# Layer-norm chunks prepared three ahead, a weight array padded to 128 rows, and the constants loaded in three parts, in a four-layer spectral kernel

## The chip, the cores and the metric

The kernel runs on one core of one Trainium2 chip, in fp32. The metric is the device time of one execution in microseconds (us), as the median of several runs. The engines are named as in the profile: PE (TensorE; PEld is its weight load), DVE (VectorE), ACT (ScalarE), POOL (GpSimd), SP (SyncE; its queue SPq issues the DMAs).

## The reference

`x` has the shape (2, 64, 64, 384). Four layers follow one another. Each takes a real 2-D FFT over the two image axes, multiplies blocks of 48 channels (8 blocks) by complex 48x48 weights twice, with an activation between, shrinks small values or not, transforms back and adds its input:

```
xf = rfft2(x)                                  # per layer
h  = act(clinear(xf, w1) + b1)                 # 8 blocks of 48 channels
y  = softshrink(clinear(h, w2) + b2)           # layers 0, 2, 3
x  = irfft2(y) + x
```

Layer 1 differs: its input is layer-normalised over the channels first, its activation is gelu, nothing is shrunk, the sum is `irfft2 + normalised x + x`, and a token MLP (384 to 1536 to 384, with a second layer norm) follows it.

## The kernel before, in words

All transforms are matmuls with constant matrices. The work unit is a **block** g of 48 channels: 8 for each layer, 32 in all. Two blocks form a **unit** of 96 channels (16 units), which is what one load of x, one store and one load of spectral weights bring. A layer-1 block is worked in 8 **steps** t, a block of the other layers in 9. A block's forward row transform f1 runs in 6 **chunks** of 8 channels, one block ahead of the rest.

PE's program is written out by hand. Step t of block g holds, in this order: m1 of step t-1 (first spectral matmul, L433), f6 (last inverse transform, L481) of an older block, f2 (forward column transform, L419) of step t, one chunk of f1 (L403) of block g+1 in the steps `f1_at` (0, 1, 3, 4, 6, 7 in layer 1), one chunk of f5 (L466) of block g-1 in the steps `f5_at` (1 to 6), and m2 of step t-1 (L449). DVE's program in a step is: the residual add of f6 (L764), the copy of m2's result to `u` (L744; L739 and L741 in the other layers), and in layer 1 `centre`.

`centre(n)` makes the normalised chunk n from x: it subtracts the mean (L796) and multiplies by the reciprocal deviation (L798), and writes slot n % 6 of the ring `xn`. Chunks 0 to 5 are made by ACT beforehand. When PE works f1 of chunk n0, DVE makes chunk n0+1 in that step, behind the `u` copy. It first waits until POOL is done with the slot: `keep(n-6)` waits for f1 of chunk n-6, multiplies the chunk by the gain (L965), adds it to x (L967) and signals `sum_ready`. Where a unit's x is needed for the first time, `centre` waits for its load too.

In layers 0, 2 and 3 POOL copies x into the ring instead (`turn`, L957), six chunks ahead of f1. POOL also prepares a unit's spectral weights (`weights`, L932 to L943, six instructions into `w0` or `w1`), in its own program order between chunks, after a wait for the load into `wstage`. That load (L275) brings the array `spectral`, which has 113 rows, to 113 partitions; the matmuls use up to 113 rows.

SP issues all DMAs from one queue, in program order. At the start: the first 128 columns of the constants (f1's matrix), the first 48 channels of unit 0 in two DMAs (`x_first`), the remaining constants, the weights of units 0 and 1, the other 48 channels of unit 0 in two DMAs, x of units 1 and 2, layer-norm rows and columns, parts of the MLP's first weights. POOL needs the other 48 channels of unit 0 for block 1, whose chunk 0 PE works in step 0 of block 0. Later, SP stores a finished unit, waits for the store, loads x three units on into the buffer, and then issues the weights load of the next unit.

Of the kernel before, what the change touches and what calls it, by code (L numbers as in the profile page):

```python
# [10 lines left out]
P = 128  # L11
BATCH, SIDE, CHANNELS = 2, 64, 384
BLOCKS, BLOCK = 8, 48
# [18 lines left out]
CHUNKS = BLOCK // CHAN  # L32
# [3 lines left out]
PART_ROWS = SIDE // PARTS  # L36
COLS = 8
RING = CHUNKS
STATS = PAIRS + 1

(C_D1, C_ID, C_D2, C_D2A, C_D2B, C_D5, C_D5H, C_D6) = [P * n for n in range(8)]
C_SIGN = 8 * P
C_COLS = C_SIGN + 5
ROWS = ONE_ROW + 1
MIX = SIDE + BLOCK
SECOND, BIAS = ROWS, ROWS + PAIR
W_COLS = BIAS + 1
# [39 lines left out]
def groups_before(g):  # L87

    return sum(LAYER[n // BLOCKS].n for n in range(g))
# [42 lines left out]
def build(nc, x, consts, spectral, lncols, ln1, cols, w1, w2, b2, out):  # L132
    with ExitStack() as ctx:
# [6 lines left out]
        def sem(name):  # L140
            return ctx.enter_context(nc.semaphore(name))
# [6 lines left out]
        const = sb("const", [P, C_COLS])  # L148
# [15 lines left out]
        with ExitStack() as scope:  # L164
# [15 lines left out]
            wstage = sb("wstage", [P, 2, 2, W_COLS])  # L180
# [30 lines left out]
        LAST_BANKS = (F5_BANK, M1_BANK)  # L211
        TURN_BANKS, MM1_BANKS, MM2_BANKS = (6, 7), (4, 5), (0, 1, 2, 3)

        s_first, s_const, s_wts = sem("s_first"), sem("s_const"), sem("s_wts")
        x_loaded = [sem(f"x_loaded{n}") for n in range(3)]
        stored = [sem(f"stored{n}") for n in range(3)]
        x_first = sem("x_first")
# [51 lines left out]
        def _(sp):  # L269

            def load_weights(unit):
                layer, i = unit // PAIRS, unit % PAIRS
                if unit >= 2:
                    sp.wait_ge(w_ready, W_STEPS * (unit - 1))
                sp.dma_start(wstage[0:ROWS, unit % 2, :, :],  # L275
                             spectral[layer].rearrange("(g k) p n -> p g k n", k=2)[:, i]
                             ).then_inc(w_loaded[unit % 2], 16)

# [5 lines left out]
            def load_unit(unit):  # L284
                for part in range(PARTS):
                    for b in range(BATCH):
                        load_rows(unit, b, part)
# [69 lines left out]
                    sp.wait_ge(m_stored[r], 16 * TILES // 2)  # L357
                load_rows(2 * PAIRS, 1, PARTS - 1)

            sp.dma_start(const[:, 0:C_ID], consts[:, 0:C_ID]).then_inc(s_first, 16)  # L360
            for n in range(2):
                sp.dma_start(xs[0][n * SIDE:(n + 1) * SIDE, :, 0:BLOCK], image(x, n, 0, SIDE, 0)[:, :, 0:BLOCK]
                             ).then_inc(x_first, 16)
            sp.dma_start(const[:, C_ID:], consts[:, C_ID:]).then_inc(s_const, 16)
            load_weights(0)
            load_weights(1)
            for n in range(2):
                sp.dma_start(xs[0][n * SIDE:(n + 1) * SIDE, :, BLOCK:PAIR], image(x, n, 0, SIDE, 0)[:, :, BLOCK:PAIR]
                             ).then_inc(x_loaded[0], 16 * PARTS)
            load_unit(1)  # L370
            load_unit(2)
            sp.dma_start(lnrow[:, :, :], ln1.rearrange("a c -> (a c)").partition_broadcast(P)
                         .rearrange("p (a c) -> p a c", a=2)).then_inc(s_wts, 16)
# [13 lines left out]
        def _(pe):  # L387
# [19 lines left out]
            def f2(g, t):  # L407

                L = layer_of(g)
                if t == 0:  # L410
                    pe.wait_ge(z_ready, CHUNKS * (g + 1))
                    if g == 0:
                        pe.wait_ge(s_const, 16)
                        pe.wait_ge(gap_clear, 1)
                start, size = L.groups[t]
                for n in range(size):
                    slot, col = L.column(start + n)
                    for a in range(2):
                        mm = pe.matmul(ps[a * SIDE:a * SIDE + BLOCK, F2_BANK, n * L.kh:(n + 1) * L.kh],  # L419
                                       z[:, g % 2, slot, :], basis(col + a * SIDE, L.kh), start=True, stop=True)  # L420
                mm.then_inc(f2_done, 1)
# [32 lines left out]
            def f5(g, k, bank=F5_BANK, reuse=1):  # L454

                L = layer_of(g)
                n = CHUNKS * g + k
                if k == 0:
                    pe.wait_ge(u_ready, groups_before(g + 1))
                    if L.norm and g % BLOCKS < 2:  # L460
                        pe.wait_ge(u_clear, 2)
                if n >= reuse:
                    pe.wait_ge(v_ready, n + 1 - reuse)
                for c in range(CHAN):
                    for a in range(2):
                        mm = pe.matmul(ps[a * SIDE:(a + 1) * SIDE, bank, c * SIDE:(c + 1) * SIDE],  # L466
                                       u[0:2 * L.kh, g % 2, k * CHAN + c, BATCH * a:BATCH * a + SPAN],
                                       const[0:2 * L.kh, (C_D5 if L.full else C_D5H) + a * SIDE:][:, 0:SIDE],
                                       start=True, stop=True)
                mm.then_inc(f5_done, 1)  # L470
# [256 lines left out]
        def _(dve):  # L727
# [82 lines left out]
            def spectral(first, last):  # L810
                norm = LAYER[first // BLOCKS].norm
                if norm:
                    centre(CHUNKS)
                for g in range(first, last):
                    L = layer_of(g)
                    for t in range(L.n):
                        done, k = rows_at(g, t)
                        if done >= first and k is not None:
                            f6(done, k)
                        if t:  # L820
                            m2(g, t - 1)
                        elif g > first:
                            m2(g - 1, layer_of(g - 1).n - 1)
                        if norm and t in L.f1_at:
                            n = CHUNKS * (g + 1 - first) + L.f1_at.index(t) + 1
                            if n < CHUNKS * (last - first):
                                centre(n)
                        if norm and 0 <= L.n * (g - last + 2) + t - 4 < HC:
                            split_first(L.n * (g - last + 2) + t - 4)
                g = last - 1  # L830
                for k in range(1, 4):
                    f6(g - 1, k)
                m2(g, layer_of(g).n - 1)
                for k in range(4, ROWCHUNKS):
                    f6(g - 1, k)
                for k in range(ROWCHUNKS):
                    f6(g, k)
# [78 lines left out]
        def _(pool):  # L916
# [79 lines left out]
            def spectral(first, last):  # L996
                for g in range(first, last):
                    for k in range(CHUNKS):
                        if layer_of(g).norm:
                            keep(CHUNKS * (g - first) + k)  # L1000
                        else:
                            turn(g, k)
                        if k == 2 and g % 2 and g > first + 1 and g + 1 < 4 * BLOCKS:
                            weights((g + 1) // 2)
                    if g == 0:
                        pool.wait_ge(s_const, 16)
                        weights(0)
                        weights(1)

            spectral(*SEGMENTS[0])  # L1010
# [15 lines left out]
def host_constants():  # L1026

    import numpy as np
    n, f = np.arange(SIDE), 2 * np.pi / SIDE
    half = np.arange(HALF)  # L1030

    col = np.stack([np.cos(f * np.outer(n, half)), -np.sin(f * np.outer(n, half))], 1)
    col[:, 1, 0] = (-1.0) ** n

    d1 = np.einsum("wak,bd->bwakd", col, np.eye(BATCH)).reshape(P, 2 * SPAN)

    inv = 2 * col.transpose(1, 2, 0)
    inv[:, 0] /= 2
    inv[1] = np.roll(inv[1], -1, 0)
    d6 = np.einsum("akw,bd->akbdw", inv, np.eye(BATCH)).reshape(P, P)  # L1040
    c, s = np.cos(f * np.outer(n, n)), np.sin(f * np.outer(n, n))
    o = np.zeros((SIDE, SIDE))
    d2 = np.block([[c, -s], [s, c]])
    d2a, d2b = np.block([[c, -s], [o, o]]), np.block([[o, o], [c, -s]])
    d5 = np.block([[c, s], [-s, c]])
    d5h = np.concatenate([d5[0:HALF], d5[SIDE:SIDE + HALF], np.zeros((SIDE, P))], 0)

    sign = np.ones((P, 5))
    sign[SIDE:SIDE + BLOCK, 0] = -1
    sign[SIDE:SIDE + BLOCK, 1:3] = -1  # L1050
    sign[ONE_ROW, 2:4] = 1 / ONE_GELU
    sign[:, 4] = -1
    return np.concatenate([d1, np.eye(P), d2, d2a, d2b, d5, d5h, d6 / SIDE, sign],
                          1).astype(np.float32)


def pack_spectral(w1, b1, w2, b2, one):

    import numpy as np
    t = np.zeros((BLOCKS, ROWS, W_COLS), np.float32)  # L1060
    for row in range(2):
        rows = slice(row * SIDE, row * SIDE + BLOCK)
        for to in range(2):
            t[:, rows, to * SIDE:to * SIDE + BLOCK] = w1[row ^ to]
            t[:, rows, SECOND + to * BLOCK:SECOND + (to + 1) * BLOCK] = w2[row ^ to]
        t[:, ONE_ROW, SECOND + row * BLOCK:SECOND + (row + 1) * BLOCK] = b2[row]
        t[:, rows, BIAS] = b1[row]
    t[:, ONE_ROW, BIAS] = one
    return t
# [50 lines left out]
```

## Time and profile before

| what | value |
|---|---|
| median of 3 runs | 2245.77 us (2243.95 to 2249.59) |
| the profiled execution's own time | 2253.02 us |
| its span in the profile | 2251.2 us |
| PE busy (matmuls) | 2075.1 us |
| DVE, ACT, POOL busy | 926.7, 874.0, 428.5 us |
| layer 0, from the first matmul | 18 to 393 us |
| layer 1 up to the MLP | 393 to 756 us |
| token MLP | 756 to 1581 us |
| layers 2 and 3 | 1581 to 2251 us |

The span begins with the first instruction. The profiled execution took 7.25 us more than the median of the runs.

### The profile page before, as it was taken

To read this page: it belongs to the slowest core of one execution; us is meant where nothing else is said; L and a number is where in the kernel's file an instruction comes from. 1 tells how busy PE (TensorE), PEld (TensorE's weight loads), DVE (VectorE), ACT (ScalarE), POOL (GpSimd) and SP (SyncE) were. 2 spreads that over 40 slices of the span, in tenths; PEclk is the share of its full clock that TensorE was granted. 3 is DMA by queue.
4 is the path that set the end of the run, shared out by engine and by line. 5 is a ranking of instruction groups with operands and counts; after the bars stand their busy time and mean duration, and the time that the engine had idled before them with its cause. 6 is when DMAs were issued, how large, how long until landed. Compare 5 with 4: busy or idle time off the path is not lost.

```text
span 2251.2 us, 76581 instructions
## 1 busy us (share of the span) xinstructions
PE 2075.1 (92%) x35424; PEld 1781.8 (79%) x35424; DVE 926.7 (41%) x1814; ACT 874.0 (39%) x1468; POOL 428.5 (19%) x425
## 2 busy tenths in 40 slices
PE   3999996788899699999999999999799999999997
PEld 2787873677776599999999999999688788878885
DVE  0354657545554333333333333332234333433443
ACT  1544445333333233333333333333344444444442
POOL 2121103744441100000000010000321210210200
PEclk8999997899999799999999999999899999999999
DMA  9615447303335200000100000004803455346214
GB/s 115 124 33 90 90 71 136 61 3 76 64 86 127 65 29 29 29 28 28 52 32 28 28 28 28 28 28 64 138 3 72 75 93 97 62 81 115 49 31 100
DMA packets 298861, 141.55 MB, mean 63 GB/s; under 512 B 275376, under 2 KB 297168, under 8 KB 298576
## 3 DMA queue, kind: packets, MB, share of 16 engines
q1 hardware_dynamic: 298576, 137.10, 31.8%
q8 instruction: 258, 4.23, 0.8%
q14 instruction: 27, 0.22, 0.0%
HBM read 74.16 MB, written 62.91 MB: 61 GB/s over the span
## 4 chain that ended last, share of the span: by engine, by line
PE 81%; issue 7%; DVE 5%; DMA 2%; SPq 2%; POOL 1%; ACT 1%; POOLq 0%; DVEq 0%; ACTq 0%
PE ps L544 18%; PE ps L559 18%; PE ps L449 9%; PE ps L403 8%; PE ps L419 7%; PE ps L433 7%; PE ps L466 7%; PE ps L481 5%; DVE xn L798 1%; DVE xn L796 1%; PE ps L529 1%; DMA wraw<-in_w 1%; DMA xs<-in_x 1%; SPq L280 1%; DMA wstage<-in_spectral 1%
## 5 line engine op out<-in xcount | busy, mean ns | idle before, releaser
L419 PEld LDWEIGHTS ps<-const,z 128*48 128x48 f32 x8384 | 287.8, 124 | 103.2 <-issue 71.1
L871 DVE TENSOR_TENSOR gl<-g,gh 128x512 fp32r<-128x512 f32 x192 | 156.8, 816 | 477.1 <-ACT gh L700 477.1
L739 DVE TENSOR_SCALAR clamp<-ps 128x384 f32<-128x384 f32 (+1 forms) x216 | 113.2, 524 | 557.3 <-PE ps L449 557.1
L697 ACT ACTIVATE g<-ps,colp 128x512 f32<-128x512 f32 x192 | 132.6, 690 | 531.3 <-PE ps L544 531.3
L403 PE MATMUL ps<-const,xn 128*64 128x64 f32 x6144 | 229.6, 229 | 107.4 <-POOL xn L957 41.3
L403 PEld LDWEIGHTS ps<-const,xn 128*64 128x64 f32 x6144 | 209.8, 144 | 111.5 <-issue 38.1
L449 PE MATMUL ps<-w,h 113*64 113x48 f32 (+1 forms) x8384 | 289.5, 220 | 7.9 <-issue 7.3
L419 PE MATMUL ps<-const,z 128*48 128x64 f32 (+1 forms) x8384 | 284.2, 218 | 7.8 <-issue 5.7
L641 ACT ACTIVATE h<-ps,w 113x512 f32<-113x512 f32 (+2 forms) x280 | 171.2, 612 | 288.8 <-PE ps L433 288.8
L449 PEld LDWEIGHTS ps<-w,h 113*64 113x64 f32 (+1 forms) x8384 | 264.3, 133 | 17.9 <-issue 12.4
L433 PE MATMUL ps<-zf,w 112*49 112x384 f32 (+5 forms) x1120 | 263.4, 533 | 1.2 <-issue 1.0
L559 PE MATMUL ps<-w2h,gh 128*128 128x384 f32 x768 | 261.8, 341 | 0.0
L559 PE MATMUL ps<-w2h,gl 128*128 128x384 f32 x768 | 258.6, 337 | 0.0
L559 PE MATMUL ps<-w2l,gh 128*128 128x384 f32 x768 | 257.5, 335 | 0.0
L481 PE MATMUL ps<-v,const 128*64 128x384 f32 x1024 | 219.8, 497 | 10.5 <-DVE xs L764 8.2
L544 PE MATMUL ps<-mth,w1l 128*128 128x512 f32 x576 | 228.3, 396 | 0.0
L544 PE MATMUL ps<-mth,w1h 128*128 128x512 f32 x576 | 225.3, 391 | 3.3 <-DVE mtl L859 3.3
L544 PE MATMUL ps<-mtl,w1h 128*128 128x512 f32 x576 | 227.9, 396 | 0.0
L957 POOL COPY xn<-xs 128x512 f32<-128x512 f32 x144 | 154.5, 1106 | 385.6 <-PE ps L403 261.4
L466 PE MATMUL ps<-const,u 128*64 128x64 f32 (+1 forms) x6144 | 221.6, 224 | 3.0 <-issue 1.9
L466 PEld LDWEIGHTS ps<-const,u 128*64 128x64 f32 (+1 forms) x6144 | 203.0, 139 | 10.3 <-issue 4.2
L596 ACT ACTIVATE z<-ps 128x512 f32<-128x512 f32 x192 | 114.9, 598 | 193.9 <-PE ps L403 193.9
(65 smaller groups left out, 2378.6 us busy)
## 6 DMA issues: line engine op xcount, KB each, us to landing
after<-xs SPq DMA_DIRECT2D x96, 384.0 KB, 5.4
xs<-after SPq DMA_DIRECT2D x96, 384.0 KB, 8.8
xm<-after SPq DMA_DIRECT2D x16, 768.0 KB, 5.8
after<-om SPq DMA_DIRECT2D x16, 768.0 KB, 4.2
out<-xs SPq DMA_DIRECT2D x32, 384.0 KB, 5.4
xs<-in_x SPq DMA_DIRECT2D x24, 384.0 KB, 8.7
xs<-in_x SPq DMA_DIRECT2D x4, 768.0 KB, 11.7
wstage<-in_spectral SPq DMA_DIRECT2D x16, 185.4 KB
```

The source lines that it names most:

```text
L403: mm = pe.matmul(ps[a * SIDE:(a + 1) * SIDE, F1_BANKS[n % 2], c * SPAN:(c + 1) * SPAN], xn[:, n % RING, c, :], basis(C_D1 + a * SPAN, SPAN ...
L419: mm = pe.matmul(ps[a * SIDE:a * SIDE + BLOCK, F2_BANK, n * L.kh:(n + 1) * L.kh], z[:, g % 2, slot, :], basis(col + a * SIDE, L.kh), start ...
L433: mm = pe.matmul(ps[rows, M1_BANK, 0:width], w[unit % 2][0:MIX, g % 2, rows], zf[0:MIX, n % 2, 0:width], start=True, stop=True)
L449: mm = pe.matmul(ps[a * L.kh:(a + 1) * L.kh, M2_BANK, c * BLOCK:(c + 1) * BLOCK], h[0:ROWS, n % 2, c * L.kh:(c + 1) * L.kh], mix[0:ROWS, g ...
L466: mm = pe.matmul(ps[a * SIDE:(a + 1) * SIDE, bank, c * SIDE:(c + 1) * SIDE], u[0:2 * L.kh, g % 2, k * CHAN + c, BATCH * a:BATCH * a + SPAN ...
L481: mm = pe.matmul(ps[a * SIDE:(a + 1) * SIDE, F6_BANKS[n % 2], 0:ROWCHUNK * BLOCK], basis(C_D6 + a * SIDE, SIDE), v[:, g % 2, rows, :].rear ...
L544: mm = pe.matmul(ps[:, MM1_BANKS[n % 2], :], a[:, at], b[:, r, k, :], start=k == 0 and m == 0, stop=k == KC - 1 and m == 2)
L559: mm = pe.matmul(ps[:, MM2_BANKS[j], 0:CHANNELS], a[:, n % 4, part], b[:, at], start=n == 0 and m == 0, stop=n == HC - 1 and m == 2)
L641: act.activation(h[0:ROWS, n % 2, 0:width], ps[0:ROWS, M1_BANK, 0:width], L.act, bias=w[g // 2 % 2][0:ROWS, g % 2, BIAS:W_COLS]).then_inc( ...
L697: act.activation(g[:, n % 2, :], ps[:, MM1_BANKS[n % 2], :], ACT.Gelu, bias=colp[:, n:n + 1]).then_inc(g_ready, 1)
L871: dve.tensor_tensor(gl[:, n % 4, :], g[:, n % 2, :], gh[:, n % 4, :], ALU.subtract).then_inc(g_low, 1)
L957: pool.tensor_copy(xn[:, n % RING], channels(g, k)).then_inc(xt_ready, 1)
```

## The change

Three things are edited. Layer 1's `centre` runs three chunks ahead of f1 instead of one: three chunks are made before block 8 and each step makes chunk n0+3. The array `spectral` gets 128 rows (the added ones are zero) and is loaded to all 128 partitions; the arithmetic on it is the same. The constants are put in another order and loaded in three parts: f1's matrix (as before), then f2's three matrices and the sign columns behind `x_first`, then the identity, f5's and f6's matrices behind the rest of unit 0. The weights load of unit 1 moves from before the rest of unit 0 to behind x of unit 1, and POOL prepares them after block 1's chunks, not after block 0's. PE waits for the third part before f5 of block 0.

```
+AHEAD = 3
-(C_D1, C_ID, C_D2, C_D2A, C_D2B, C_D5, C_D5H, C_D6) = [P * n for n in range(8)]
-C_SIGN = 8 * P
-C_COLS = C_SIGN + 5
+SIGNS = 5
+C_D1, C_D2, C_D2A, C_D2B, C_SIGN = [P * n for n in range(5)]
+C_ID, C_D5, C_D5H, C_D6, C_COLS = [C_SIGN + SIGNS + P * n for n in range(5)]
...
-                sp.dma_start(wstage[0:ROWS, unit % 2, :, :],
+                sp.dma_start(wstage[:, unit % 2, :, :],
...
-            sp.dma_start(const[:, 0:C_ID], consts[:, 0:C_ID]).then_inc(s_first, 16)
+            sp.dma_start(const[:, 0:C_D2], consts[:, 0:C_D2]).then_inc(s_first, 16)
             for n in range(2):
                 sp.dma_start(xs[0][n * SIDE:(n + 1) * SIDE, :, 0:BLOCK], ...
-            sp.dma_start(const[:, C_ID:], consts[:, C_ID:]).then_inc(s_const, 16)
+            sp.dma_start(const[:, C_D2:C_ID], consts[:, C_D2:C_ID]).then_inc(s_second, 16)
             load_weights(0)
-            load_weights(1)
             for n in range(2):
                 sp.dma_start(xs[0][n * SIDE:(n + 1) * SIDE, :, BLOCK:PAIR], ...
+            sp.dma_start(const[:, C_ID:], consts[:, C_ID:]).then_inc(s_const, 16)
             load_unit(1)
+            load_weights(1)
             load_unit(2)
...
 (PE, f2, g == 0)
-                        pe.wait_ge(s_const, 16)
+                        pe.wait_ge(s_second, 16)
 (PE, f5, k == 0)
+                    if g == 0:
+                        pe.wait_ge(s_const, 16)
...
 (DVE, spectral)
-                    centre(CHUNKS)
+                    for n in range(CHUNKS, CHUNKS + AHEAD):
+                        centre(n)
...
-                            n = CHUNKS * (g + 1 - first) + L.f1_at.index(t) + 1
+                            n = CHUNKS * (g + 1 - first) + L.f1_at.index(t) + AHEAD
...
 (POOL, spectral)
                     if g == 0:
-                        pool.wait_ge(s_const, 16)
+                        pool.wait_ge(s_second, 16)
                         weights(0)
+                    if g == 1:
                         weights(1)
...
 (host)
-    t = np.zeros((BLOCKS, ROWS, W_COLS), np.float32)
+    t = np.zeros((BLOCKS, P, W_COLS), np.float32)
```

## Rows read from the trace of the kernel before

**Rows 1.** The page, part 1: busy time of each engine

```profile
PE 2075.1 (92%) x35424; PEld 1781.8 (79%) x35424; DVE 926.7 (41%) x1814; ACT 874.0 (39%) x1468; POOL 428.5 (19%) x425
```

**Rows 2.** Busy time by stretch, with granted clock, DMA share and GB/s last

```profile
27.10:46.17 19.07, 0.00 (x0) 0.00 (x1) 0.00 (x0) 0.49 (x1) 3.65 (x10) 0.55 0.92 115
...
393.40:712.00 318.60, 279.94 (x7442) 233.58 (x7442) 166.79 (x219) 118.41 (x227) 153.45 (x114) 0.95 0.32 62
...
1620.00:2238.00 618.00, 602.73 (x15082) 504.64 (x15078) 248.79 (x407) 278.15 (x462) 99.19 (x117) 1.00 0.38 67
```

**Rows 3.** Timeline of SP's queue, the first two weights loads: start, us

```profile
12.59 8.23 SPq L275 DMA_DIRECT2D wstage<-in_spectral  x2
```

**Rows 4.** Timeline of POOL in the first 64 us, with its idle time before

```profile
16.48 6.17 POOL L957 COPY xn<-xs 128x512 f32<-128x512 f32 x6 [15.63 <-DMA xs<-in_x]
...
25.75 0.40 POOL L932 TENSOR_TENSOR w<-wstage,const 112x128 f32<-112x128 f32 x1 [3.09 <-DMA wstage<-in_spectral]
...
36.62 0.40 POOL L932 TENSOR_TENSOR w<-wstage,const 112x128 f32<-112x128 f32 x1 [8.93 <-DMA wstage<-in_spectral]
...
45.07 6.12 POOL L957 COPY xn<-xs 128x512 f32<-128x512 f32 x6 [6.50 <-DMA xs<-in_x]
...
63.08 3.16 POOL L957 COPY xn<-xs 128x512 f32<-128x512 f32 x3 [11.90 <-DMA xs<-in_x]
```

**Rows 5.** The page, part 6: DMA issues, KB each, us to landing

```profile
xs<-after SPq DMA_DIRECT2D x96, 384.0 KB, 8.8
...
wstage<-in_spectral SPq DMA_DIRECT2D x16, 185.4 KB
```

**Rows 6.** A unit's weights load in layer 0: SP, two stretches, POOL, PE

```profile
202.94 0.52 SPq L275 DMA_DIRECT2D wstage<-in_spectral  x1
...
210.00:220.00 10.00, 7.80 (x183) 6.00 (x181) 3.86 (x6) 3.43 (x6) 3.60 (x8) 1.00 0.05 16
...
216.40 0.40 POOL L932 TENSOR_TENSOR w<-wstage,const 112x128 f32<-112x128 f32 x1 [46.89 <-DMA wstage<-in_spectral]
...
219.40 1.47 PE L403 MATMUL ps<-const,xn 128*64 128x64 f32 x32 [2.20 <-POOL xn L957]
```

**Rows 7.** PE's waits in layers 2 and 3: us in total, times, longest

```profile
PE ps L403 <- POOL xn L957: 2.0, 4, 0.7
```

**Rows 8.** PE's waits in layer 1

```profile
PE ps L403 <- DVE xn L798: 32.9, 26, 2.3
```

**Rows 9.** Timeline of PE and DVE in two steps of layer 1

```profile
509.94 0.87 PE L419 MATMUL ps<-const,z 128*48 128x32 f32 x32
510.64 1.13 PE L403 MATMUL ps<-const,xn 128*64 128x64 f32 x32
...
518.72 1.06 DVE L796 TENSOR_TENSOR xn<-xs,mv 128x512 f32<-128x512 f32 x1
519.81 1.90 DVE L798 TENSOR_TENSOR xn<-xn,rstd 128x512 f32<-128x512 f32 x1
...
521.77 1.15 PE L403 MATMUL ps<-const,xn 128*64 128x64 f32 x32 [1.65 <-DVE xn L798]
```

**Rows 10.** Durations (ns, min/median/max) of a chunk's instructions on DVE (last) and POOL

```profile
L798 DVE TENSOR_TENSOR xn<-xn,rstd x42: 691/693/1965, 400.2 to 677.2; 128x512 f32<-128x512 f32 x42
L965 POOL TENSOR_TENSOR xn<-xn,lnrow x48: 1034/1044/1955, 395.5 to 679.2; 128x512 f32<-128x512 f32 x48
L967 POOL TENSOR_TENSOR xs<-xs,xn x48: 1575/1623/2913, 396.6 to 680.3; 128x512 f32<-128x512 f32 x48
```

**Rows 11.** Busy time in two blocks of layer 1, columns as in rows 2

```profile
521.80:561.20 39.40, 35.05 (x960) 28.93 (x960) 21.78 (x30) 15.12 (x29) 17.84 (x12) 1.00 0.51 101
561.20:604.50 43.30, 37.88 (x962) 30.94 (x962) 22.66 (x30) 15.11 (x29) 21.53 (x18) 0.92 0.44 64
```

**Rows 12.** SP's queue at the load of unit 7

```profile
550.21 1.31 SPq L294 DMA_DIRECT2D after<-xs  x2
556.28 13.99 SPq L280 DMA_DIRECT2D xs<-after  x8
```

More of the change, by code:

```diff
@@ L212, in build @@
         TURN_BANKS, MM1_BANKS, MM2_BANKS = (6, 7), (4, 5), (0, 1, 2, 3)
-        s_first, s_const, s_wts = sem("s_first"), sem("s_const"), sem("s_wts")
+        s_first, s_second, s_const, s_wts = sem("s_first"), sem("s_second"), sem("s_const"), sem("s_wts")
         x_loaded = [sem(f"x_loaded{n}") for n in range(3)]
@@ L1046, in host_constants @@
     d5h = np.concatenate([d5[0:HALF], d5[SIDE:SIDE + HALF], np.zeros((SIDE, P))], 0)
-    sign = np.ones((P, 5))
+    sign = np.ones((P, SIGNS))
     sign[SIDE:SIDE + BLOCK, 0] = -1
@@ L1052, in host_constants @@
     sign[:, 4] = -1
-    return np.concatenate([d1, np.eye(P), d2, d2a, d2b, d5, d5h, d6 / SIDE, sign],
+    return np.concatenate([d1, d2, d2a, d2b, sign, np.eye(P), d5, d5h, d6 / SIDE],
                           1).astype(np.float32)
```

## The prediction

> **What bounds the kernel now.** I read the page's first part (which engine is full), then the busy time by stretch (where it is not), then who PE waits for in each stretch, then the timeline around the longest waits. PE's matmuls fill 2075 of 2251 us [rows 1], the next engine 927, so only two things are worth time: PE's idle time, and stretches at a lower granted clock. Three kinds of idle time touch the change. At the start PE stands for 19.07 us, from 27.10 to 46.17 [rows 2]; its next work is f1 of block 1, and POOL starts to copy for it at 45.07, when the second half of unit 0 has landed [rows 4]. In layer 1, PE waits 26 times for `centre`, 32.9 us in all [rows 8], at a mean clock of 0.95, where layers 2 and 3 have 1.00 [rows 2]. And at units' weights loads POOL stands still until the load lands and PE then waits for POOL [rows 6, 7].
>
> **The weights load, and its padding.** The load issued at 202.94 is used at 216.40, and from 210 to 220 the DMA engines are 0.05 busy at 16 GB/s [rows 6]: that is one engine of 16. At the start it looks the same: the two loads are issued from 12.59 on [rows 3], one is ready by 25.75 and the other at 36.62 [rows 4], 10.87 us apart, so 185.4 KB [rows 5] at 17 GB/s. With 113 rows the load runs on one DMA engine. That the 128-row form uses all is not in this trace. The x loads, whose partitions come in 64s, ran at 115 GB/s [rows 2], and 210 KB (185.4 x 128/113) at that rate are 1.9 us. The bounds for the padded load are thus 1.9 us (all engines) and 12.3 us (one engine, 10.87 x 128/113). I take the lower end, since the nearest loads have a row count with the factor 16. The Trainium skill ("DMA: Bandwidth & Descriptors", section "Why a DMA increments its semaphore by 16 and not by 1") says a DMA uses the largest number of engines up to 16 that divides its outer dimension: 113 would get one, 128 sixteen. By that rule the 0.05 share is one engine, the trace agrees, and the estimate is the lower end; no run here yet shows the 128.
>
> **Start.** The first half of unit 0 is in by 16.48, behind it come in the new order 194.5 KB of constants, 210 KB of weights and 1536 KB of x (64 x 64 pixels x 48 channels x 4 bytes, twice). That is 1.99 MB, at 115 GB/s 17.3 us, so it lands at 33.7; larger packets in the first 400 KB may save 2 us. I take 33. Before it was 45.07: **minus 12**, bounds 10 and 14. What is late next: POOL's copy for block 2 was possible at 63.08 [rows 4], but PE asks for that chunk only in step 0 of block 1, a whole block (9 steps, over 30 us) after it resumes, so x of unit 1, which also lands some 11 us earlier, has over 15 us in hand. The weights of unit 1 now come behind it, and `weights(1)` (six short instructions on POOL, the first 0.40 us [rows 4], so 2 to 3 us) stands before the first copy of block 2; both fit into that slack. The third part of the constants (256 KB, 2.3 us) is ahead of unit 1 and is needed only in block 1, step 2. I cost these at nothing; if the slack were gone, the price would be the sum, 5 us.
>
> **Layer 1.** Where PE is not stopped, f1 starts 0.70 us after f2 (509.94 to 510.64), while f2 is drawn 0.87 long [rows 9]: each wait is really 0.17 longer. 32.9 + 26 x 0.17 = 37.3 us. The waits lie where two f1 steps are adjacent: DVE begins L796 only after the `u` copy, so 1.06 + 1.90 us come after PE's m2 [rows 9]. Three ahead, that chain has over two steps of time, and f1 finds its chunk ready. What is new is that `centre(n0+3)` needs `keep(n0-3)` where before it needed `keep(n0-5)`. A step of layer 1 without waits is 4.3 us (a block of 39.4 [rows 11] less 37.3 / 7 = 5.3 of waits, over 8 steps), so three f1 steps are at least 12 us; keep takes 1.0 for L965 and 1.6 to 2.9 for L967 [rows 10], so there is room, also behind a `weights` of 3 us. Only at the beginning there is none: `centre(8)` and `centre(9)` wait for `keep(2)` and `keep(3)`, and behind them on DVE stand the first `u` copies, for which PE's m2 waits. POOL delivers a chunk each 3.3 us or so, DVE makes one in 3, and block 8 has no f5 and hardly any f6 to cover it. I count 3 us lost there. The load of unit 7 is asked for two f1 steps earlier: it is issued from 556.28, its last piece at 568.5 [rows 12], plus 8.8 us [rows 5] gives 577. It is asked for at step 4 of block 12, which lies six to seven unstopped steps (28 to 30 us) behind the residual that releases the store at 550.21 [rows 12]: 578 to 580. Cost 0, at worst 3 us.
>
> **The clock.** 318.6 us at 0.95 [rows 2] are 32 us at the lower level (0.5). A block without a dip takes 39.4 us, one at 0.92 takes 43.3 [rows 11]: 6.9 us at the lower level cost 3.9. All 32 would cost 18; some falls into waits which I have counted, so 11. The dips lie only in the stretch in which PE stands in most steps, so I expect them gone. Layer 1: 37.3 + 11 - 3 = **minus 45**, bounds 30 (no clock back, more lost on DVE) and 50.
>
> **DVE against POOL.** L798 takes 0.69 alone and up to 1.97 beside POOL, L967 1.58 alone and up to 2.91 [rows 10]: they hold each other up. Taken alone a chunk costs 1.05 + 0.69 + 1.04 + 1.58 = 4.36 us of both; 6 chunks are 26 us of a block that will take 34 (above), so they fit on average. The Trainium skill ("SBUF — State Buffer", section "SBUF: two separate sides") calls the port pair of DVE and GpSimd an exclusive lock, the loser fully blocked; the trace agrees in kind (+1.2 us on one side). By it, in the steps that have f1 but no f5 (34.1 us less 12 matmul groups of 1.1, over 8 steps, plus one group: 3.7 us of PE), the pair falls 0.66 us behind each, and the gain would be at most 6 us smaller.
>
> **Weights loads in the steady state.** Waits for POOL: 2.2 us once [rows 6], 2.0 us in layers 2 and 3 in four waits [rows 7], 5 x 0.17, and the lower clock behind the first of them (L403 there 1.47 us [rows 6], 1.13 otherwise [rows 9], and the matmuls behind it likewise; I take 2): 7 us. With the load in some 9 us earlier, POOL has done all before PE asks. Part of PE's waits for its own instructions may lie under the long load as well; I count 1. **Minus 8**, bounds 2 and 9. At the MLP's start PE waits for stores and loads of x, and I count nothing.
>
> **Sum.** 12 + 45 + 8 = 65. From the profiled execution's 2253.0 that gives 2188, and it lay 7.25 above the median: 2245.8 - 65 = **2180.8**.
>
> **Rivals.**
> - *The waits go, the clock does not come back.* In its favour: the dips in layer 1 are not all beside a long wait. Then layer 1 gives 34 and the sum is 54: 2192. Chance 0.13.
> - *DVE and POOL fall behind each other*, so waits move from f1 to m2: layer 1 gives 30, the sum is 50: 2196. The average load speaks against it. Chance 0.09.
> - *The padding changes nothing*, the load stays at one engine. Then the second half of unit 0 waits for one such load instead of two (gain about 8) and the steady state gives 0: 8 + 45 = 53, 2193. For it: no row shows a 128-row weights load. Chance 0.04.
> - *Slower: DVE stands in every step for POOL's `keep`.* If `centre` had to wait for the keep just begun (2.6 us) each of 42 times, and m2 stood behind it, 109 us would be added against 65 gained: 2290. It decides once POOL lags by more than three f1 steps, 12 us; in layer 1 POOL is busy 153 of 319 us [rows 2]. Chance 0.02.
> - Forecast as above: 0.72.
>
> **Range and chances.** Each term at its low bound gives 42 (2204), each high 73 (2173). The likeliest case alone covers 2173 to 2192; with the rivals and some room for the one run that the rows come from, 2168 to 2206. A difference of 0.3% (7 us) is what can be told from no change. Faster 0.96, same 0.02, slower 0.02.
>
> **What the profile will show.** PE idle from 27 to about 34 instead of 46; POOL's L957 at 33. The weights used within 3 us of the x loads' end and no stretch at 16 GB/s. No waits of PE for L798, a block of layer 1 at 34 to 35 us, clock 0.99 or more there. Wrong would be: PE's waits for `u` (L744) in layer 1, DVE waiting for L967 beyond block 8 or for unit 7's load, or L932 still waiting 10 us and more.

## The result, and the profile after

The changed kernel takes **2187.88 us** (median of 4 runs, 2183.46 to 2192.85) against 2246.44 us for the kernel before (median of 4 runs): a ratio of 0.974, 95% interval 0.971 to 0.976, or 58.6 us less. 2180.8 was forecast (range 2168 to 2206), 65 us less. The profiled execution had a time of 2183.46 us and a span of 2181.6 us. It is the fastest of its four runs, while the one profiled of before was slower than its median, so the two profiles differ by 69.6 us, 11 us more than the medians do. Stages below are compared profile with profile; what the whole change is worth is the 58.6.

Where the 69.6 us lie, as read from the timelines of PE (start of the first f1 after the rest of unit 0 is in; first f1 of block 8; start of the last f6 run of layer 1; first transpose of the MLP; span):

| | before | after | stage shorter by |
|---|---|---|---|
| PE resumes | 46.17 | 28.96 | 17.2 |
| layer 1 begins (f1 of block 8) | 393.42 | 371.31 | 4.9 |
| last f6 of layer 1 | 721.81 | 656.59 | 43.1 |
| MLP begins | 750.22 | 684.90 | 0.1 |
| span | 2251.2 | 2181.6 | 4.3 |

In the page of the kernel after, part 1 answers to [rows 1]. PE has 18 us less of busy time for the same 35424 matmuls, which is the clock, and DVE and POOL have 12 us more each. Nearly all of that lies in layer 1, where their instructions overlap more and lengthen each other (the rows of the layer below, third and fifth busy time):

```profile
PE 2056.9 (94%) x35424; PEld 1765.7 (81%) x35424; DVE 939.3 (43%) x1814; ACT 873.8 (40%) x1468; POOL 440.3 (20%) x425
```

The start, in POOL's timeline of the kernel after (it answers to [rows 4]; columns are start, duration, line, what, and idle time before with its releaser):

```profile
16.60 6.09 POOL L962 COPY xn<-xs 128x512 f32<-128x512 f32 x6 [15.74 <-DMA xs<-in_x]
22.73 0.40 POOL L937 TENSOR_TENSOR w<-wstage,const 112x128 f32<-112x128 f32 x1
...
27.87 6.19 POOL L962 COPY xn<-xs 128x512 f32<-128x512 f32 x6 [3.20 <-DMA xs<-in_x]
46.74 0.40 POOL L937 TENSOR_TENSOR w<-wstage,const 112x128 f32<-112x128 f32 x1 [12.68 <-DMA wstage<-in_spectral]
...
48.64 4.12 POOL L962 COPY xn<-xs 128x512 f32<-128x512 f32 x4
```

The first half of unit 0 is in at 16.6 as before. The weights of unit 0 are there when POOL comes to them (no wait at L937), and the other half is in at 27.87 and not at 45.07. The busy time of that stretch, with clock, DMA share and GB/s in the last three columns, first in the kernel after, then in the kernel before (the share adds up the times of packets, and can pass 1):

```profile
17.00:28.00 11.00, 9.24 (x216) 8.99 (x216) 0.00 (x0) 3.84 (x7) 7.76 (x13) 1.00 1.37 195
```

```profile
17.00:45.00 28.00, 8.74 (x216) 8.48 (x216) 0.00 (x0) 4.08 (x7) 9.56 (x18) 0.71 0.60 80
```

195 GB/s against 80: the same queue, once the loads of 113 rows are gone from it. The bytes are not all the same: in the kernel after the 195 also hold the third part of the constants (256 KB) and the first of unit 1. In the kernel before, the first load of 113 rows is nearly alone in flight from 18 to 28, with the second half of unit 0 still behind it:

```profile
18.00:28.00 10.00, 8.41 (x216) 8.12 (x212) 0.00 (x0) 4.08 (x7) 6.61 (x11) 1.00 0.08 24
```

Five profiles have the start of the kernel after (it, and `e5`, `e6`, `e7` and `e10` below). Their second half of unit 0 is in at 26.3 to 30.2 us, and PE resumes at 27.4 to 31.3, so 17.2 is one draw from 15 to 19.

In layer 1, who PE waits for from 367 to 720 us of the kernel after (total, times, longest; it answers to [rows 8]; the waits for `issue`, PE's own instructions, and for the MLP's first rows are left out):

```profile
PE ps L405 <- ACT xn L611: 11.7, 1, 11.7
...
PE ps L451 <- DVE u L758: 0.6, 1, 0.6
...
PE ps L451 <- DVE u L748: 0.3, 1, 0.3
```

Of the 26 waits for `centre` (now L802) none is left, and two small ones for the first `u` copies have come. The steps around the end of block 10, of which [rows 9] showed step 6 and the stalled step 0 of block 11; here steps 7, 0 and 1 in PE's timeline:

```profile
469.55 0.87 PE L421 MATMUL ps<-const,z 128*48 128x32 f32 x32
470.25 1.13 PE L405 MATMUL ps<-const,xn 128*64 128x64 f32 x32
...
473.94 1.13 PE L405 MATMUL ps<-const,xn 128*64 128x64 f32 x32
...
477.63 1.13 PE L405 MATMUL ps<-const,xn 128*64 128x64 f32 x32
```

f1 follows f2 by 0.70 us, and neighbouring f1 are 3.69 us apart where they were 5.5. The six gaps of such a block are 4.77, 3.70, 3.69, 8.58, 4.77 and 8.59: 34.1 us. How that comes out in busy time and clock over the whole layer, in before and in after:

```profile
393.40:721.80 328.40, 289.05 (x7648) 240.26 (x7648) 169.58 (x224) 121.99 (x233) 155.40 (x120) 0.95 0.34 67
```

```profile
371.30:656.60 285.30, 275.57 (x7649) 230.81 (x7650) 181.74 (x224) 122.17 (x234) 167.60 (x120) 0.98 0.39 78
```

PE's idle time falls from 39.4 to 9.7 us, its busy time by 13.5 us.

A weights load of layer 0, in SP's queue and POOL's timeline of the kernel after (it answers to [rows 6]):

```profile
183.71 2.02 SPq L276 DMA_DIRECT2D wstage<-in_spectral  x1
```

```profile
191.12 0.40 POOL L937 TENSOR_TENSOR w<-wstage,const 112x128 f32<-112x128 f32 x1 [40.82 <-DMA wstage<-in_spectral]
```

7.4 us from issue to use where it was 13.5 (202.94 to 216.40). The way from issue to use is 6.1 us shorter; the DMA engines work on the x loads issued just before, at a share of 1.3, until 188. Over the whole kernel PE's waits for POOL's copies are down to the first two of the start:

```profile
PE ps L405 <- POOL xn L962: 19.0, 2, 17.8
```

### The profile page after: what moved, and what is told of

The parts are those of the page before. It is cut to its first block, busy times and chain, and to the rows that moved or that the text cites. A ratio compares the mean times of both kernels' runs of the same rounds, so it can differ in the third digit from the quotient of the medians.

```text
span 2181.6 us, 76583 instructions
## 1 busy us (share of the span) xinstructions
PE 2056.9 (94%) x35424; PEld 1765.7 (81%) x35424; DVE 939.3 (43%) x1814; ACT 873.8 (40%) x1468; POOL 440.3 (20%) x425
## 4 chain that ended last, share of the span: by engine, by line
PE 91%; issue 3%; DVE 2%; DMA 1%; SPq 1%; ACT 1%; POOL 0%; POOLq 0%; DVEq 0%; ACTq 0%
PE ps L563 18%; PE ps L548 18%; PE ps L451 11%; PE ps L421 10%; PE ps L435 10%; PE ps L470 8%; PE ps L405 8%; PE ps L485 7%; PE ps L533 1%; DMA wraw<-in_w 1%; DMA xs<-in_x 1%; DVE st L780 0%; DVE mv L785 0%; DVE xn L800 0%; DVE xn L802 0%
## 5 line engine op out<-in xcount | busy, mean ns | idle before, releaser
L451 PE MATMUL ps<-w,h 113*64 113x48 f32 (+1 forms) x8384 | 285.9, 218 | 10.7 <-issue 9.7
L622 ACT ACTIVATE zf<-ps 112x512 f32<-112x512 f32 (+1 forms) x216 | 121.4, 562 | 149.6 <-PE ps L421 149.2
```

The costliest lines, as they stand in the source:

```text
L451: mm = pe.matmul(ps[a * L.kh:(a + 1) * L.kh, M2_BANK, c * BLOCK:(c + 1) * BLOCK], h[0:ROWS, n % 2, c * L.kh:(c + 1) * L.kh], mix[0:ROWS, g ...
```

## The experiments

### Each part alone

`e1` is the kernel before with the three places of `centre` changed (`AHEAD = 3`):

```
-                    centre(CHUNKS)
+                    for n in range(CHUNKS, CHUNKS + AHEAD):
+                        centre(n)
...
-                            n = CHUNKS * (g + 1 - first) + L.f1_at.index(t) + 1
+                            n = CHUNKS * (g + 1 - first) + L.f1_at.index(t) + AHEAD
```

> The kernel before with centre three ahead and nothing else. Theory (the three parts are independent, and layer 1 gave 43 of the gain): about 43 us less than before, ratio 0.981, no wait of PE for L802's counterpart, granted clock of layer 1 at 0.98 or more, start as before (PE resumes at 46). Rival (part of layer 1's gain came from the faster weights loads): 35 us less or under.

Measured: 2210.81 us against 2248.85, ratio 0.984 (0.982 to 0.987), 38 us less. PE resumes at 44.16, no wait for `centre` is left, and layer 1 (394.32 to 681.80) is 287.5 us long, 40.9 less than before. The ratio's interval (30 to 41 us less) reaches the rival's 35, so the median does not decide; the stage does: 40.9 of the 43.1 us are there without padding. PE resumes 2 us earlier than in the kernel before, though the loads are the same: the start scatters by that much.

`e2` is the kernel before with the padding alone:

```
-                sp.dma_start(wstage[0:ROWS, unit % 2, :, :],
+                sp.dma_start(wstage[:, unit % 2, :, :],
...
-    t = np.zeros((BLOCKS, ROWS, W_COLS), np.float32)
+    t = np.zeros((BLOCKS, P, W_COLS), np.float32)
```

> The kernel before with 128 rows in the weights array and nothing else. Theory (a weights load of 113 rows runs on one DMA engine and holds up what is queued behind it; the start's gain belongs to the padding): PE resumes at 30 to 32 us instead of 46.2, the unit loads' weights are in within 3 us of x, 22 us less in all, ratio 0.990. Rival (the order of the constants gave the start's gain): PE resumes at 40 or later, 10 us less in all.

Measured: 2222.48 us, ratio 0.989 (0.986 to 0.992), 26.4 us less. PE resumes at 32.77, 13.4 us earlier. So the start's gain is mostly the padding's. From 20 to 30 us the second half of unit 0 is nearly alone in the queue of `e2`; last columns as above:

```profile
20.00:30.00 10.00, 7.31 (x182) 7.02 (x178) 0.00 (x0) 3.95 (x7) 6.71 (x15) 1.00 1.41 137
```

At a share of 1.41 it moves 137 GB/s, in runs of 192 bytes. From 32 to 45, with whole units in runs of 384 bytes, the same queue moves 187 at 1.31.

`e3` is the other side of both, the kernel after with `AHEAD = 1` and 113 rows, so that only the order of the loads and the three parts are new:

```
-AHEAD = 3
+AHEAD = 1
...
-                sp.dma_start(wstage[:, unit % 2, :, :],
+                sp.dma_start(wstage[0:ROWS, unit % 2, :, :],
...
-    t = np.zeros((BLOCKS, P, W_COLS), np.float32)
+    t = np.zeros((BLOCKS, ROWS, W_COLS), np.float32)
```

> The kernel after with centre one ahead and the weights array at 113 rows: only the order and the three parts of the constants. Theory (one long load on one engine still stands before the rest of unit 0): PE resumes at 38 to 41, 6 us less in all, ratio 0.997. Rival (the order gives the start's gain): PE resumes at 32 or before, 14 us less.

Measured: 2244.27 us, ratio 0.9985 (0.9967 to 1.0003): no difference that can be told. PE resumes at 37.59, 8.6 us earlier, and loses it again. Its rows show where. POOL gets the weights of unit 1 at 63.21, and then the row of ACT and the row of PE:

```profile
81.70 0.84 ACT L660 ACTIVATE w1h<-wraw 128x768 fp32r<-128x768 f32 x1 [6.84 <-DMA wraw<-in_w]
```

```profile
83.17 1.50 PE L451 MATMUL ps<-w,h 113*64 113x48 f32 x32 [4.32 <-ACT h L645]
```

ACT, in its program order, waits 6.8 us for the first part of the MLP's weights (`wraw`), the activation `h` stands behind it, and PE's m2 waits 4.3 us for `h`. Why `wraw` is late is in SP's queue, first of `e3`, then of the kernel after (start, duration of the issuing, line):

```profile
47.48 1.26 SPq L276 DMA_DIRECT2D wstage<-in_spectral  x1
48.78 23.95 SPq L281 DMA_DIRECT2D xs<-in_x  x8
...
76.37 23.13 SPq L308 DMA_DIRECT2D wraw<-in_w  x6
```

```profile
38.78 1.90 SPq L276 DMA_DIRECT2D wstage<-in_spectral  x1
40.72 14.98 SPq L281 DMA_DIRECT2D xs<-in_x  x8
...
59.22 26.55 SPq L308 DMA_DIRECT2D wraw<-in_w  x6
```

Behind the 113-row load the issuing of unit 2's x takes 23.95 us, behind the 128-row load 14.98, and `wraw` goes out at 76.4 where it went out at 59.2. PE is 9 us behind the kernel after there, `wraw` is 17. In the kernel before `wraw` goes out at 77.1, and ACT waits for it at most 2.4 us: `e3` brings PE and ACT 8.6 us forward and `wraw` by 0.7. I had not thought of this wait for either kernel; in the kernel after, ACT's waits at that line are 0.6 to 2.3 us and reach no matmul.

### The number of rows

`e4` and `e9` are the kernel after with 127 and with 116 rows (the lines are those of `e4`; `e9` has 116 in both places):

```
-                sp.dma_start(wstage[:, unit % 2, :, :],
+                sp.dma_start(wstage[0:127, unit % 2, :, :],
...
-    t = np.zeros((BLOCKS, P, W_COLS), np.float32)
+    t = np.zeros((BLOCKS, 127, W_COLS), np.float32)
```

> The kernel after with 127 rows in the weights array, loaded to 127 partitions, in place of 128. Theory (the number of rows decides how many DMA engines take part; 127 is prime, so one): the load takes 12 us again, PE resumes at 38 to 41, in all 15 us more than the kernel after, near 2203. Rival (bytes or the share of partitions matter, not the divisor): as the kernel after, near 2188, PE resumes at 29.

> The kernel after with 116 rows (4 x 29) in the weights array, loaded to 116 partitions. Theory (the largest divisor of the row count up to 16 sets the number of DMA engines, here 4): 190 KB at 4 times the 17 GB/s of one engine, 2.8 us a load; PE resumes at 30 to 31, no wait of POOL's weights over 5 us behind the x loads is left on PE's path, at most 4 us more than the kernel after. Rival (only a multiple of 16, or all 128 partitions, goes fast): as with 127 rows, 24 us more, PE resumes at 35.

With 127 rows: 2212.41 us, ratio 0.985 (0.983 to 0.987), 24.5 us over the kernel after. With one row less than 128 almost the whole worth of the padding is gone. A load of layer 0 and its use, in SP's and POOL's timelines of `e4`, and the DMA engines meanwhile:

```profile
198.34 0.52 SPq L276 DMA_DIRECT2D wstage<-in_spectral  x1
```

```profile
213.26 0.40 POOL L937 TENSOR_TENSOR w<-wstage,const 112x128 f32<-112x128 f32 x1 [48.40 <-DMA wstage<-in_spectral]
```

```profile
208.00:213.00 5.00, 5.00 (x134) 4.11 (x132) 2.59 (x5) 2.13 (x4) 0.00 (x0) 1.00 0.08 23
```

14.9 us from issue to use at a DMA share of 0.08. PE resumes at 35.30, 3 us before the stretch that I had given, and it meets the same wait behind `wraw` as `e3`, 7.8 us long. Beyond the start PE also waits seven times for POOL's copies, 10.9 us in all, where the kernel after has no such wait. With the 6.3 us by which PE resumes later, these come to 25, against 24.5 measured; the 15 us expected lacked the wait behind `wraw`.

With 116 rows (4 x 29): 2191.49 us, ratio 0.973 (0.971 to 0.976), within 4 us of the kernel after. From issue at 191.02 to use at 198.68 are 7.7 us. PE resumes at 32.44 (30 to 31 was expected), and behind `wraw` its m2 waits 3.1 us. At its end the load is nearly alone, and its speed can be read:

```profile
196.00:198.00 2.00, 1.78 (x61) 1.77 (x62) 0.00 (x0) 0.97 (x2) 0.00 (x0) 1.00 0.36 97
```

97 GB/s at a share of 0.36, against 23 at 0.08 for 127 rows: four times as much. 116 rows are closer to 113 than to 128 in bytes and in share of partitions, and the whole behaves like 128: it is the divisor and not the size. The Trainium skill ("DMA: Bandwidth & Descriptors", section "Why a DMA increments its semaphore by 16 and not by 1") says that the largest number up to 16 that divides the outer dimension sets the engines, 1 for 113 and 127, 4 for 116, 16 for 128; the four row counts agree with it, and the factor of four between 127 and 116 rows too. That 128 rows use all 16 is not read by itself, since their load never runs alone for long.

### How far ahead

`e5` is the kernel after once more, `e6` and `e7` are the kernel after with two and five in place of three, `e8` has padding and three ahead in the old order of loads. They ran on one chip. `e5` and `e8` have no new lines (`e8` is the edits of `e1` and `e2` together); the others:

```
-AHEAD = 3
+AHEAD = 2        # e6
+AHEAD = 5        # e7
```

> The kernel after, unchanged, beside the next three on the same chip: near 2188 us, ratio 0.974 to before.

> The kernel after with centre two chunks ahead in place of three. Theory (a chunk needs only to be made before the step of its f1, so one step of room is enough): as the kernel after within 0.2%, no wait of PE for L802, a block of layer 1 at 34.1 us. Rival (DVE and POOL fall behind each other in the four neighbouring f1 steps, and the room of three chunks is what hides it): PE waits of 0.3 to 1 us at the third and fourth of those steps, 5 to 15 us more.

> The kernel after with centre five chunks ahead, so that chunk n0+5 needs keep of n0-1, the chunk that PE worked one f1 step ago. Theory (POOL is fast enough: keep takes 2.6 to 3.6 us, a step with f1 at least 3.7): DVE waits for L972 about 1 us in the neighbouring f1 steps, hidden in later steps, 3 us more at most beside the start of layer 1, where five chunks stand before the first u copy (5 to 8 us more). In all 5 to 12 us more than the kernel after. Rival (DVE standing for keep holds up the u copy in each step and PE with it): 40 us or more over the kernel after.

> The kernel after with the old order of loads and the constants in two parts: padding and three ahead only. Theory (with the padding in, the order moves only 256 KB of constants and 210 KB of weights from before the rest of unit 0): PE resumes at 32.8, where padding alone had it, 4 us more than the kernel after, 2192. Rival (the order gives more than it shows at the start): 8 us or more over the kernel after.

| | median us | ratio to before | layer 1, us |
|---|---|---|---|
| e5, three | 2185.93 | 0.972 (0.969 to 0.974) | 288.2 |
| e6, two | 2184.81 | 0.971 (0.969 to 0.974) | 284.3 |
| e7, five | 2198.86 | 0.978 (0.975 to 0.980) | 298.0 |
| e8, old order | 2189.77 | 0.973 (0.971 to 0.976) | 287.5 |

Two ahead is as good as three (1 us, inside the noise), with the same 34.1 us for a block and no wait of PE for DVE in layer 1. The rival that three chunks of room hide a backlog of DVE and POOL falls.

Five ahead costs 13 us, a little over the 5 to 12 expected, and its rows show two places. At the beginning of layer 1 DVE makes five chunks and the sixth before the first `u` copy; PE's m2, in its timeline, waits for that copy:

```profile
399.43 1.50 PE L451 MATMUL ps<-w,h 113*32 113x48 f32 x32 [10.68 <-DVE u L758]
```

And DVE asks for unit 7's x before it is in; the row of DVE, and the row of PE behind it:

```profile
534.00 1.60 DVE L800 TENSOR_TENSOR xn<-xs,mv 128x512 f32<-128x512 f32 x1 [8.06 <-DMA xs<-after]
```

```profile
538.61 0.94 PE L451 MATMUL ps<-w,h 113*32 113x48 f32 x32 [2.71 <-DVE u L748]
```

DVE waits for POOL's `keep` (L972) once in `e7`, 10.2 us at its first chunk, and that wait is in the kernel before too (10.3 us). After it there is none, not even the 1 us in neighbouring steps that the theory had, though each chunk needs the keep of a chunk only one f1 step back. What costs at the beginning is DVE's own work: beside POOL a chunk takes it 3.7 us (L800 1.8, L802 1.9), so the first `u` copy starts at 398.2, where it starts at 390.9 in the kernel after.

`e8` is 3.8 us over `e5`, as expected; PE resumes at 32.37. The intervals overlap: the order's worth on top of the padding is at the edge of what can be told.

### Padding and order without more room

`e10` is the kernel after with `AHEAD = 1`.

> The kernel after with centre one chunk ahead, as before the change: padding and order alone. Theory (the parts add up): 2248 less 26 for the padding less 4 to 5 for the order, near 2217, 30 us over the kernel after or a little more; 33 us of waits for L802 and a clock of 0.95 to 0.96 in layer 1. Rival (part of layer 1's gain needs the padding): 40 us or more over the kernel after.

Measured: 2225.56 us, ratio 0.988 (0.986 to 0.990), 37.7 us over the kernel after (2187.88), 33.4 us of waits for `centre`. Three ahead is worth 38 us in the kernel before (`e1`) and 38 here; with each kernel set against the kernel before of its own occasion it is 33 to 37 here. The parts add up only roughly: 38 for three ahead, 26 for the padding, 4.6 (with an interval that reaches 0) for the order make 69 against 59 to 62 measured together. Each part has an interval of 4 to 7 us to either side, so the 7 to 10 us over can be scatter or a small overlap of the parts; the runs do not tell which. The figure of 2217 was 8.5 too low, because `e10` is 3 us slower than `e2`, which has no new order, where I expected it 5 faster (against their own kernels before the two are equal, 0.988 and 0.989). The order by itself is worth nothing that can be told with one chunk ahead. The rival of 40 us or more is not seen; and `e1` has its 38 us without the padding.

## Why the prediction was right

**The weights load.** The step that chose between 1.9 us and 12.3 us was right, shown by 113, 127, 116 and 128 rows. The load and its landing are 7.4 us from issue to use, part of that behind the x loads, so the weights came 6.1 us earlier and not 9; the rival "the padding changes nothing" is excluded.

**Start, minus 12, measured 17.2.** The mechanism was right, the term was mis-sized. "at 115 GB/s 17.3 us" took the rate of the stretch from 27.10 to 46.17 [rows 2], and that stretch was itself held back by the 113-row loads that the change removes (it falls to 16 GB/s from 36 to 38, about the landing of the second). Freed of them the 1.99 MB took 11.3 us (16.6 to 27.9), or 176 GB/s, in the profile of the kernel after, and 9.7 to 13.4 us in the four others with the same start. The 195 GB/s of the stretch are not the rate of the x loads alone, which `e2` shows at 137. A rate read from a stretch in which the removed cost still acts is a bound, not a value. `e2` shows 13.4 of the 17.2 us for the padding alone; with PE resuming at 44.2 in `e1` as well, the scatter of this stage is some 2 us on either side. The costs taken as nothing were nothing: x of block 2 is copied at 48.64 and PE asks for it at 61.

**Layer 1, minus 45, measured 43.1.** Idle time fell by 29.6 us and busy time by 13.5, together 43.1. Of the forecast, 37.3 for the waits counted 26 x 0.17 = 4.4 us that the profile books as busy, so in its terms it was 32.9 less 3 lost = 29.9 of idle time (29.6 measured) and 11 + 4.4 = 15.4 of busy time (13.5). The block of 34.1 us came out to the tenth. The 3 us for the beginning had the wrong mechanism: `centre(8)` and `centre(9)` never waited for `keep`, and PE's waits for `u` were 0.9 us (in `e7`, where five chunks stand in front, 10.7). PE's waits for its own instructions in the layer rose from 4.5 to 7.1 us, which the sum did not have; that the idle time agrees to 0.3 us is luck. That DVE's two instructions and POOL's get in each other's way is true and grew, with no cost: L802's median went from 0.69 to 1.91 us and L972's from 1.62 to 2.14 (the two rows below answer to [rows 10]), and both stayed inside a block of 34 us. The estimate of up to 6 us less, from the exclusive lock, is not borne out: layer 1 gave 1.9 us less than forecast, and no block shows DVE falling behind.

```profile
L802 DVE TENSOR_TENSOR xn<-xn,rstd x42: 691/1906/1972, 378.0 to 599.5; 128x512 f32<-128x512 f32 x42
```

```profile
L972 POOL TENSOR_TENSOR xs<-xs,xn x48: 1592/2142/2625, 374.5 to 615.1; 128x512 f32<-128x512 f32 x48
```

**The clock.** It came back from 0.95 to 0.98 and not to 0.99 or more. The step that did not hold is "I expect them gone": the dips do not all come from the waits for `centre`. What is left is at the layer's beginning, where PE waits 11.7 us for ACT in both kernels (clock 0.76 and 0.83 from 370 to 390), and at one place near 522 us, where PE waits 1.58 and 1.07 us for its own instructions while unit 7's x is loaded, and its clock falls behind that:

```profile
515.04 1.03 PE L470 MATMUL ps<-const,u 64*64 64x64 f32 x27 [1.58 <-issue]
...
520.89 0.33 PE L470 MATMUL ps<-const,u 64*64 64x64 f32 x3 [1.07 <-issue]
...
523.07 1.50 PE L485 MATMUL ps<-v,const 128*64 128x384 f32 x4
```

f6 takes 1.50 us there and 0.81 otherwise. The same gap (here 13.4 us between two f1 that are 8.6 apart elsewhere) is in `e1` and `e5` to `e8`, 12.2 to 14.4 us wide, and in the kernel before (12.5 us, at 567), so the change did not bring it. That the other dips of before came from the waits for `centre` is shown by `e1` and `e10`: 0.98 without the waits against 0.95 in the kernel before, and 0.95 with them against 0.98 in the kernel after, other things as they were. The row of layer 1 in `e10`:

```profile
375.40:703.30 327.90, 289.00 (x7650) 240.26 (x7650) 169.28 (x224) 122.08 (x234) 156.06 (x120) 0.95 0.34 68
```

**Weights loads in the steady state, minus 8.** Layer 0 after the start is 4.9 us shorter, the MLP and layers 2 and 3 together 4.3: 9.2. PE's waits for POOL's copies beyond the start are gone, as the sum had them. The other runs bear out only the part in layer 0: from PE's resuming to block 8 it takes 339 to 345 us in the seven profiles with 128 rows, and 347 and 350 in the kernel before and `e1`. The MLP and layers 2 and 3 take 1496.2 to 1500.9 us with 128 rows, 1501.0 in the kernel before and 1496.9 in `e1`, so no gain there can be told from scatter. PE's waits for its own instructions, which were 37 us in the profile before and 41 after, are part of that scatter.

**The sum.** 12 + 45 + 8 = 65; the profiles show 17 + 43 + 9 = 69.6, the medians 58.6. The last step took the difference of two profiled runs for that of the medians. The profile of before lies 7 us above its median (2253.0 to 2245.8), that of after 4 us below (2183.5 to 2187.9), so some 11 us of the 69.6 are scatter, and the forecast of 65 lies between the two measures. In the profiles the start came out 5 us larger than forecast and layer 1 some 2 smaller. "The waits go, the clock does not come back" and "DVE and POOL fall behind each other" are excluded; the range held.

## What to carry to other kernels

Look at the row count of each small load: a prime one (113, 127) ran at 16 to 24 GB/s when nearly alone, a DMA share of 0.05 to 0.08, which is about one engine of 16, and held up what stood behind it in the queue; padding to 128 gave that back, and 116 nearly all of it. Where a producer stands behind other work in its engine's program, one more step of lead was enough here (two ahead did what three did), and too much lead costs at the segment's first block, where the produced chunks stand before everything, and at loads that are asked for earlier. Do not price a stretch by a rate that was measured while the removed cost still acted, and look which other loads a mean rate holds.

## What the runs showed of the hardware that was not expected

The x loads in runs of 192 bytes moved 137 GB/s at a DMA share of 1.41 (`e2`, 20 to 30 us), those in runs of 384 bytes 187 GB/s at 1.31 (32 to 45 us). A DMA of 113 rows also delays later ones of 64 or 128 partitions, and the queue's issuing with them: 23.95 us for eight x loads against 14.98, and for the two x loads behind the first weights load 14.98 us with 113 rows (`e3`), 14.94 with 127, 9.85 with 116 and 6.50 with 128. In the new order of loads ACT then waited 6.8, 9.1 and 4.3 us for the first `wraw` with 113, 127 and 116 rows; with 128 rows no wait there is over 2.3 us, and neither is one over 2.4 in the kernel before with its 113 rows and old order. DVE's L802 and POOL's L972 slow each other to almost three times and 1.3 times their time alone, at no cost that can be seen in blocks of 34.1 us; at the beginning of layer 1, where `u` stands behind DVE's chunks, the same slowing is part of the 10.7 us of `e7`.
